# A hybrid block on one core: attention, output projection and last FFN written as one straight program

## What is computed

```python
x = x + scan(layernorm(x))              # selective scan, state 16 per feature
x = x + ffn(layernorm(x))               # "f1"
q, k, v = rope(x_n @ Wq + bq), rope(x_n @ Wk + bk), x_n @ Wv + bv    # x_n = layernorm(x), 16 heads of 16
scores = einsum('bhqd,bhkd->bhqk', q, k) / 4
x = x + (softmax(scores) @ v) @ Wo + bo
x = x + ffn(layernorm(x))               # "f2"
# ffn(x) = sqrt((x @ cos(theta + theta_noise))**2 + (x @ sin(phi + phi_noise))**2)
```

## Time and profile before

| | |
|---|---|
| time, median of 3 | 3761.28 us (3759.84 to 3768.51) |
| the profiled execution | 3761.9 us, span 3760.2 us |
| granted TensorE clock, mean | 0.964 of full speed |
| PE busy | 3472.7 us (92%), 22853 instructions |
| DVE busy | 3393.0 us (90%), 5278 instructions |
| ACT busy | 2582.1 us (69%) |
| POOL busy | 606.2 us (16%) |
| all instructions | 77817 |

### The profile page before, as it was taken

How to read it: one execution, slowest core, us unless ns; L and a number is a source line. 1 busy time by engine, 2 the same in 40 slices (tenths; PEclk the granted TensorE clock), 3 DMA queues, 4 the chain that set the end, 5 groups by cost and what they waited for, 6 DMA issues and landing times. The chain is left out here.

```text
span 3760.2 us, 77817 instructions
## 1 busy us (share of the span) xinstructions
PE 3472.7 (92%) x22853; PEld 1321.2 (35%) x22880; DVE 3393.0 (90%) x5278; ACT 2582.1 (69%) x4673; POOL 606.2 (16%) x436
## 2 busy tenths in 40 slices
PE   6688887885999999999999999999999999999988
PEld 3122222440233333333333333333333333333334
DVE  5899998785999999999999999999999999999616
ACT  5444443470488887888788788878878887878844
POOL 2689897071000000000000000000000000000020
PEclk9899999995799999999999999999999999999999
DMA  1000000152101001010101101010100101010011
GB/s 60 1 1 1 0 0 0 55 119 40 26 3 29 15 18 29 3 28 3 29 6 28 29 3 28 3 29 3 29 27 6 29 3 29 3 29 5 3 54 45
DMA packets 49398, 80.10 MB, mean 21 GB/s; under 512 B 12400, under 2 KB 39536, under 8 KB 44912
## 3 DMA queue, kind: packets, MB, share of 16 engines
q1 hardware_dynamic: 48496, 73.99, 8.3%
q10 hardware_dynamic: 512, 1.05, 0.2%
HBM read 53.37 MB, written 21.23 MB: 20 GB/s over the span
## 5 line engine op out<-in xcount | busy, mean ns | idle before, releaser
L1450 DVE TENSOR_REDUCE part_max<-max_scores 128x1 f32<-128x512 f32 x4096 | 2545.4, 684 | 111.1 <-PE max_scores L1260 45.0
L1423 ACT ACTIVATE prob<-scores 128x512 f32<-128x512 f32 x4096 | 2115.8, 603 | 621.6 <-PE scores L1296 619.3
L1296 PE MATMUL scores<-q_rows,k_rows 64*128 64x512 bf16 x4096 | 1283.5, 382 | 0.0
L1303 PE MATMUL scores<-q_rows,k_rows 35*128 35x512 bf16 x4096 | 1233.9, 380 | 0.0
L1340 PE MATMUL acc<-prob,v_ones 128*32 128x512 f32 x8192 | 1095.8, 607 | 0.0
L1260 PE MATMUL max_scores<-k_twin,q_twin 64*128 64x512 bf16 x2048 | 801.3, 391 | 56.3 <-DMA k_twin<-qk_parts 49.7
L1263 PE MATMUL max_scores<-k_rows,q_rows 64*128 64x512 bf16 x2048 | 801.9, 392 | 32.0 <-issue 18.8
L1263 PEld LDWEIGHTS max_scores<-k_rows,q_rows 64*128 64x128 bf16 x2048 | 189.8, 93 | 929.0 <-DVE part_max L1450 855.7
L1296 PEld LDWEIGHTS scores<-q_rows,k_rows 64*128 64x128 bf16 x4096 | 381.7, 93 | 294.4 <-PE scores L1303 24.0
L1303 PEld LDWEIGHTS scores<-q_rows,k_rows 35*128 35x128 bf16 x4096 | 378.3, 94 | 187.2 <-ACT prob L1423 38.8
L1192 POOL COPY v_ones<-v_all 128x512 f32 (+1 forms) x16 | 9.7, 609 | 2436.3 <-PE acc L1340 2436.2
(11 more groups left out here) (121 smaller groups left out, 1420.3 us busy)
## 6 DMA issues: line engine op xcount, KB each, us to landing
qk_parts<-roped_parts SPq DMA_DIRECT2D x64, 192.0 KB, 2.9
q_rows<-qk_parts SPq DMA_DIRECT2D x192, 64.0 KB
k_rows<-qk_parts SPq DMA_DIRECT2D x180, 64.0 KB
q_twin<-qk_parts SPq DMA_DIRECT2D x128, 64.0 KB
x_res<-in_x SPq DMA_DIRECT2D x4, 1024.0 KB, 9.0
rope_trig<-in_trig SPq DMA_DIRECT2D x4, 1024.0 KB, 9.3
att_t<-acc_sb SPq DMA_DIRECT2D x128, 32.0 KB
att_all<-att_t SPq DMA_DIRECT2D x8, 512.0 KB, 9.0
```

Source lines behind the costliest of these rows:

```text
L1296: return nc.tensor.matmul(sc[:, n % SB, :], k_rows[0:LANE, par, kt * P:(kt + 1) * P], q_rows[0:LANE, par, q0:q0 + CH], start=(j == 1), sto ...
L1303: return nc.tensor.matmul(sc[:, n % SB, :], k_rows[LANE:KM, par, kt * P:(kt + 1) * P], q_rows[LANE:KM, par, q0:q0 + CH], start=(j != 1), s ...
L1423: nc.scalar.activation(prob[:, t % PBUF, j * CH:(j + 1) * CH], sc[:, n % SB, :], ACT.Exp, scale=SCALE).then_inc(exp_done, 1)
L1450: nc.vector.tensor_reduce(part_max[:, t, c:c + 1], mx[:, unit_bank(h, half, u), :], AXX, ALU.max).then_inc(dve_read, 1)
```

## The change

Nothing that the reference asks for is computed in another way but the order of a few sums. These are the parts.

- **No loops.** `ends_apart` becomes a Python loop and `heads` is gone: all heads are written out, in every stage. Waits compare with constants, and `wait_apart` is a plain wait.
- **One block.** Attention, output projection and "f2" are one block. While the last half runs, SP loads the weighted values and sums of queries 0 to 2047 (`load_weighed(0)`), DVE inverts their sums, PE puts eight `recip_row` products into eight of the last half's steps, and POOL adds the bias early. After the last `weigh` PE projects the first eight units of two tiles, then spreads the other half's reciprocals, then runs the FFN with the other eight `out_unit`s between its first units.
- **First half.** Its maxima are taken in groups of four banks, one DVE reduce of 128x4x512 each (L1489 is the narrow one, L1506 the wide one), with eight banks in two groups. `qk_parts` has another layout, so that a head's part is one DMA of 16 rows where two of 8 rows were; and the first units wait only for the rows that they read (`first_loaded`).
- **Split and turn.** DVE keeps only the reduce to `neg_max` (now L1500), which it does after unit 0 of the next half. POOL makes the three parts; `part_max` is double-buffered. The turn stands one unit later (TURN_AT = 7), behind `weigh`, and ACT copies it to `max_rows` after the four exponentials of step 29.
- **Last half.** From there on, with no max units beside, a chunk's scores are one matmul over all 99 rows (`score`, L1304) in place of two.

The diff, cut to its core:

```diff
 def ends_apart(eng, n, body):
     body(0, True, False)
-    with eng.Fori(1, n - 1) as i:
+    for i in range(1, n - 1):
         body(i, False, False)
     body(n - 1, False, True)
-def wait_apart(eng, sem, value, passed):
-    eng.wait_ge(sem, value)
-    eng.sem_inc(passed, 1)
...
-TURN_AT = 6
+TURN_AT = 7
+RECIP_FROM = 12
...
-        mem.qk_parts = nc.dram_tensor("qk_parts", [2, NPART, 2, D // 2, S], BF16, kind="Internal").ap()
+        mem.qk_parts = nc.dram_tensor("qk_parts", [2, NPART, D // 2, 2, S], BF16, kind="Internal").ap()
...
-        attention(nc, mem)
+        attention(nc, mem, io, out)
         attn.close()
-        attention_output(nc, mem, io)
-        ffn(nc, mem, "f2", out)
...
-        def heads(eng, body):
-            body(0, 0, True, False)
-            with eng.Fori(0, (H - 2) // 2) as pair:
-                body(2 * pair + 1, 1, False, False)
-                body(2 * pair + 2, 0, False, False)
-            body(H - 1, 1, False, True)
```

More of the change, by code:

```diff
@@ L826, in _ @@
                     sp.sem_inc(trig_here, 1)
-                with sp.Fori(0, NC) as i:
+                for i in range(0, NC):
                     for n in range(NU):
@@ L1167, in head @@
                         store(h - 1, 1)
-                    move_max(h, 1, par)
+                    move_max(h, 1)
                     store(h, 0)
-                    if not last:
-                        move_max(h + 1, 0, 1 - par)
-                load_rows(sp, q_rows, 0, 0, Q_SLOTS, 0, 0)
-                load_rows(sp, q_twin, LANE, 0, Q_TWIN, 0, 0)
-                move_max(0, 0, 0)
-                heads(sp, head)
-                store(H - 1, 1)
-                for s in stored:
-                    sp.wait_ge(s, 16 * 5 * H)
+                    if h < H - 1:
+                        move_max(h + 1, 0)
@@ new lines, in second_half, with weigh @@
+                def second_half(h, t, j):
+                    if j == 1:
+                        pe.wait_ge(half_low, h * STEPS + (t + 1))
+                        score_high(h, t, j).then_inc(s_high, 1)
+                    else:
+                        pe.wait_ge(half_high, h * (3 * STEPS) + (3 * t + max(j, 1)))
+                        score_low(h, t, j).then_inc(s_low, 1)
+                def weigh(h, t):
+                    half, kt = t // NKT, t % NKT
+                    if t == 0:
+                        pe.wait_ge(v_ready, h + 1)
+                    if kt == 0 and 2 * h + half > 0:
+                        pe.wait_ge(acc_read, 2 * h + half)
+                    pe.wait_ge(exp_done, h * (4 * STEPS) + 4 * t + 4)
+                    for i in range(4):
+                        last = nc.tensor.matmul(acc[32 * i:32 * i + VW, :], v_ones[:, h % 2, kt, :],
+                                                prob[:, t % PBUF, i * CH:(i + 1) * CH], start=(kt == 0),
+                                                stop=(kt == NKT - 1), tile_position=(0, 32 * i))
+                    last.then_inc(pv_done, 1)
@@ new lines, in row_max @@
+                def row_max(b):
+                    parts = part_max[:, b % 2, :, :] if b > 0 else part_max[:, 0, :, 0:NC // WIDE]
+                    if b > 0:
+                        dve.wait_ge(dve_read, units_done(b, MAXU - 1))
+                        dve.wait_ge(neg_ready, b)
+                    else:
+                        dve.wait_ge(first_read, MAXU // WIDE)
+                    nc.vector.tensor_reduce(neg_max[:], parts, AXX, ALU.max, negate=True).then_inc(low_ready, 1)
+                dve.wait_ge(ones_set, 3)
@@ new lines, in _ @@
+                add_out(1)
+                dve.wait_ge(o_added, 1)
+                units.dve_stats(dve, 0)
+                add_out(2)
+                dve.wait_ge(o_added, 2)
+                units.dve_stats(dve, 1)
+                add_out(3)
+                dve.wait_ge(pv_done, H * STEPS)
+                units.dve_normalise(dve, 0)
+                add_out(4)
+                units.dve_normalise(dve, 1)
+                add_out(5)
+                reciprocals(1)
+                for i in range(6, NU_F // 2):
+                    add_out(i)
@@ L1591, in hybrid_kernel @@
+                units.dve_add_amp(dve, NU_F - 1)
 def hybrid_kernel(nc, io, out):
```

1002 lines of the change are left out of this document (445 added, 557 removed).

## The result

The changed kernel took 3602.93 us, median of 4 runs (3601.08 to 3604.05), beside 3763.24 for the kernel before (3759.84 to 3768.51). The ratio is 0.9572, with a 95% interval of 0.9556 to 0.9589: 160 us less, where 140 were forecast and the range reached from 3592 to 3662.

A forecast was written before the change was run, and what follows sets the result against it. PE and DVE, both nearly full, were taken to hold each other in a ring. Terms -37 - 43 - 18 - 6 - 3 - 6 - 27 = -140 us, and 3761.9 - 140 - 0.6 = 3621 us; range 3592 to 3662.

The forecast's parts named there:

- The 29 periods: Attention from the second move of the maxima (SP) to the 31st; forecast 80 us less.
- The back jumps: Attention's loop of seven rounds: six jumps back at 6.2 us each vanish in straight code; -37 us.
- The slower rival: Straight program's instructions don't arrive in time, eating 140 us in 15 heads, 9.3 a head; chance 0.03.
- The late turn: POOL's split or ACT's copy delays SP's move past the first scores; 30 to 75 us lost, 3651 to 3696; chance 0.1.
- Between two halves: DVE sheds split (0.74) and turn's copy (0.43 + 0.16), plus straight-code pace: 1.45 us in 30 halves; -43, bounds 0 and -55.
- The ring: PE and DVE alternate in attention; rival: PE holds the pace, so 43 becomes 10, time 3654 us; chance 0.2.
- Load: Before attention's first product: fewer rows awaited, DMAs of twice the rows; -18 us, bounds -12 and -24.
- first product 16 to 24 us after the loads begin: Sign expected in the profile after: attention's first product starts that long after its loads begin.
- First half: Attention's first 128 max units: DVE reduces over four banks save three starts of four; -6 us, bounds 0 and -10.
- Ahead of attention: Stages before attention lose their loops and counting waits; -3 us, bounds +2 and -8.
- Last half: Attention's last half: four fewer score matmuls a step save 13 us, eight reciprocal products return 7; -6, bounds 0 and -13.
- Tail: From the last `weigh` to the end: projection units overlap storing, loading, inverting; 108.4 against 134.65 us; -27, bounds -15 and -32.

The follow-up runs named there:

- loops_only: Kernel before with all hardware loops written out in Python, counting waits kept; 3710.51 us, ratio 0.9860.
- turn_ahead_of_weigh: Changed kernel with split and copy of the turned maxima on DVE and the turn one unit earlier (TURN_AT = 6), ahead of the weighing; 3640.88 us, ratio 0.9680.
- split_and_turn_on_dve: Changed kernel with the split and the copy of the turned maxima back on DVE, turn still behind the weighing; 3630.07 us, ratio 0.9650.
- early_row_max: Changed kernel with split and copy on DVE, and reduce to the negated maximum plus split ahead of the next half's unit 0; 3632.57 us, ratio 0.9654.
- split_on_dve: Changed kernel with the four splitting operations back on DVE, right behind the reduce to the negated maximum; 3630.23 us, ratio 0.9651.
- two_part_scores: Changed kernel with two score matmuls a chunk (35 and 64 rows) in the last half too, in the old order; 3614.67 us, ratio 0.9613.
- tail_in_line: Changed kernel with the projection's first eight units behind the second half's reciprocal products instead of ahead of them; 3620.20 us, ratio 0.9622.

## Why the prediction was right, and where it wasn't

The time lay in the range, 18 us under the forecast, and all terms but two came within 3 us of their figures. The 29 periods gave 90.6 for 80, and of the parts of that term one was near by chance. The runs split it so:

| part of the 29 periods | us | from |
|---|---|---|
| loops written out | -45.5 | before to loops_only |
| turn behind the weighing | -11.0 | turn_ahead_of_weigh to split_and_turn_on_dve |
| reduce to the negated maximum behind unit 0 | -3.1 | early_row_max to the same |
| split on POOL | -24.3 | split_on_dve to after |
| turn's copy on ACT | -0.7 or -0.2 | with the split on DVE, on POOL |
| left over | -6 | loops_only to turn_ahead_of_weigh, less the 3.1 |

*The back jumps, right in size and half right in cause.* 37 us for six jumps were forecast and 4 for the pace of straight code; written-out loops gave 45.5. In the loop an ordinary period is 81.81 in the mean and in straight code 81.26, so I should have taken the whole 0.55 and not a quarter of 0.5. The prediction put what a jump costs beyond PE's 3.8 us of waiting to the refilling of the ring. That step fails: the waits for issue are 2.3 to 3.8 us, 18.8 in all six, and after them PE ran 34 us at half clock. In loops_only 3 x 3.4 us at half clock lengthened three periods by 4.8 us in all, so 34 us cost an estimated 16, and 18.8 and 16 make 34.8 of the 35.6 us that the six long periods have over 81.81. The same falls are most of what is left over in the table. The slower rival fell: in the 2600 us of attention the waits of PE and its weight loads for issue have one of 4.3 us, and the others are 0.8 or less. The late turn fell too: PE and ACT wait nowhere in the periods for the moved rows, though the prediction's own terms (0.5, 1.85 and 2) left 0.65 us of slack and not 1.

*Between two halves, right in size and wrong in what it named.* Split: 0.74 forecast, 0.84 measured. The copy of the turn: 0.43 + 0.16 forecast, about nothing measured, in two pairs of runs with the turn behind the weighing. The step that failed read the copy's 0.43 us in the earlier trace rows as DVE time on the path, when DVE would have waited for PE at the turn anyway; the 0.16 us of waiting for PE behind the copy, in the same rows, is the sign of it. What gave 0.38 in its place is the turn's position on PE, which was listed as a part of the change and had no price in the prediction. The 0.38 is shown, and the rows of turn_ahead_of_weigh show the chain of waits behind it. Not run is the turn at its old place with ACT's copy; there DVE idles 0.47 us behind a copy of 0.21, so the copy should cost nothing there either.

*The ring.* The prediction said that PE and DVE hold each other. Half shown: DVE's pause of 0.83 comes through whole, yet with 0.27 us taken off every reduce a half falls by 1.5 us only, because PE's own work fills 78.4. In the kernel before, a half of 81.8 had 3.4 us over PE's own 78.4; now 1.5 are left.

*Load, -18 forecast, -20.5 measured.* The layout's part is shown, 10.3 us. In the prediction the rate of 16-row DMAs was open between two bounds, and it came out near the one for twice the rate: 1.02 of the engines and 129 GB/s against 0.50 and 88. The rate grew less than the share, and 129 GB/s over 12.9 us are 1.67 MB where 1.31 were counted, so rows that nobody waits for take a part of the engines. The sign "first product 16 to 24 us after the loads begin" missed, and by the prediction's own bounds it should have read 9 to 21. The Trainium skill ("DMA: Bandwidth & Descriptors", Why a DMA increments its semaphore by 16 and not by 1) says that a DMA is dealt to the largest number of engines up to 16 that divides its rows, 8 and 16 here, and both shares agree with it. That the kernel with its loops written out and the old loads starts 27.1 and not 33.4 us after them is not explained: the same bytes move at 87 GB/s instead of 70, at a share of 0.46 and 0.48. It is one trace of each, and no run isolates it.

*First half, -6 and -6.1.* A wide reduce is 2.2 us as guessed, 4 x 0.598 less 0.2.

*Ahead of attention, -3 forecast, -7.5 measured in this pair of traces.* The size is not settled. The ten variants whose code ahead of attention is that of the changed kernel start attention's loads at 847.3 to 853.3, 849.3 in the median, and the changed kernel's 846.9 is the earliest of all. So some 5 us are likely, and the 0.5 us between before (854.4) and loops_only (853.9) is less than this scatter and tells nothing of the loops there.

*Last half, -6 and -6.2.* Merged scores give 12 (two_part_scores), and the eight reciprocals' products take 5.8 back: from the last move to the end of the last `weigh` it is 89.9 us in two_part_scores, which has them, and 84.1 before.

*Tail, -27 and -29.4.* The prediction's own terms make 134.65 - 108.4 = 26.3 and not 27. The order in which the projection covers the last store, load and inversion is worth 17 us, 10 of them the wait and the rest that PE's clock would have been at half behind it, a cost that the prediction did not have. The reciprocals were ready 0.65 us after the eight units, but not because the chain is that long: in tail_in_line it takes 10.4 us, and the eight units cover 14.1. In the changed kernel DVE comes to the reciprocals at 3505.39 only, 7.0 us after SP issues the load of the sums (3498.36), where it is 2.7 in tail_in_line (3501.19 to 3503.91), since additions and passes of the FFN stand ahead of them in its order.

## What to carry to other kernels

Where two engines feed each other through a few buffers, price a move on both: an instruction that you take off one may have stood in a wait that stays, and where a small one stands in front of the partner's long one may be worth more than who does it. To see what is left, take work from one engine without touching the other; here it showed that PE alone needs 78.4 of 79.9 us, so that a faster DVE can give at most about 1.5 us a half. A wait of PE can cost nearly twice its length when the clock falls during it (9.7 us of waiting and 8.2 of clock in tail_in_line, 18.8 and an estimated 16 in the six back jumps), so fill it with products rather than shorten it. Where one stretch is longer than its twins, look at its granted clock first.

## What the runs showed of the hardware

In tail_in_line a wait of PE of 10.4 us brings the granted clock to 0.50, from 3 us into the wait to 16.6 us after it. Each of the six back jumps of the kernel before makes PE wait 2.3 to 3.8 us for issue and is followed by 3.4 to 6.8 us at half clock. Straight code can have such a fall as well: three of 29 halves of loops_only are 1.6 us longer by 3.4 us at half clock, with PE as busy ahead of it as in a half without one. Reads of 8 rows load half of the DMA engines' time and reads of 16 rows all of it. Two more changes of PE between 64-row tiles and column tiles in a step, with the half-sized products that they part, cost 0.41 us.
